# Decay factors through device memory in a gated delta-rule tower on one TensorE

## The reference

```python
h = tokens(x)                                  # patches @ W + b, class token first
z = layernorm(h)                               # factor r = 1 / sqrt(var + 1e-5), one for each token
q, k, v = silu(conv4(z @ Wq)), silu(conv4(z @ Wk)), silu(conv4(z @ Wv))
alpha, beta = sigmoid(z @ Wa), sigmoid(z @ Wb) # one of each for each token
for t in tokens:                               # state S: 128 x 128 for each image
    S = alpha[t] * (S - beta[t] * (S @ k[t]) k[t]^T) + beta[t] * v[t] k[t]^T
    o[t] = S @ q[t]
h = h + (rmsnorm(o) * silu(z @ Wg)) @ Wo       # q and k are l2-normed
h = h + ffn(layernorm(h))                      # mixed weights, about the last 200 us
```

## Time and profile before

| | |
|---|---|
| three executions, us | 844.44, 844.86, 850.1 (median 844.86) |
| the profiled execution, us | 845.34 |
| its span, first to last instruction, us | 843.3 |
| outside the span, us | 2.04 |
| PE busy | 819.7 us, 97% |
| DVE, ACT, POOL busy | 77%, 59%, 43% |
| start of the gates in step -1, 0 and 1, us | 23.18, 38.04, 60.03 |
| step 11, from level 1 of the inverse to that of step 12 (L1325 to L1325), us | 24.16 |

### The profile page before, as it was taken

One profiled execution on the slowest core, in us unless ns is written; L12 is line 12 of the kernel. 1 busy time (PEld: TensorE's weight loads), 2 busy tenths in 40 slices (PEclk: granted clock), 3 DMA queues, 4 the chain that ended last, 5 costly groups with the idle time before them and its releaser, 6 DMA issues.

```text
span 843.3 us, 31784 instructions
## 1 busy us (share of the span) xinstructions
PE 819.7 (97%) x12142; PEld 650.3 (77%) x12142; DVE 646.1 (77%) x2314; ACT 499.5 (59%) x1773; POOL 364.8 (43%) x530
## 2 busy tenths in 40 slices
PE   9899999999999999999999999999998999999996
PEld 7777787787877877878778778787787777777775
DVE  5467888888888888888888888888785977777434
ACT  1446565666766656567666566666644466666664
POOL 3123433333344233333442332333312398888775
PEclk7999999999999999999999999999999999999999
DMA  2001112222211011011111111111012133333331
GB/s 67 16 13 29 42 53 61 58 51 63 63 50 46 26 37 34 25 38 38 36 35 27 35 35 26 38 33 33 28 53 75 51 113 113 113 113 113 113 113 45
DMA packets 78661, 45.37 MB, mean 54 GB/s; under 512 B 20357, under 2 KB 69803, under 8 KB 78511
## 3 DMA queue, kind: packets, MB, share of 16 engines
q1 hardware_dynamic: 77663, 42.80, 18.2%
q10 hardware_dynamic: 848, 0.54, 0.2%
HBM read 23.69 MB, written 19.63 MB: 51 GB/s over the span
## 4 chain that ended last, share of the span: by engine, by line
PE 92%; DVE 5%; issue 2%; ACT 1%; POOL 0%; DVEq 0%; ACTq 0%; POOLq 0%
PE bank L2174 10%; PE bank L2148 9%; PE bank L1412 7%; PE bank L1413 5%; PE bank L1325 5%; PE bank L1349 5%; PE bank L1368 3%; PE bank L1506 3%; PE bank L1483 3%; PE bank L1542 3%; PE bank L1435 3%; PE bank L1369 3%; PE bank L1561 3%; PE bank L1517 2%; PE bank L1474 2%; PE bank L1546 2%
## 5 line engine op out<-in xcount | busy, mean ns | idle before, releaser
L2174 PEld LDWEIGHTS bank<-work 128*128 128x128 f32 x768 | 89.6, 192 | 12.0 <-issue 11.8
L2046 ACT ACTIVATE work<-bank,b1mix 128x512 f32<-128x512 f32 x96 | 65.7, 688 | 54.9 <-PE bank L2148 54.9
L2174 PE MATMUL bank<-work 128*128 128x128 f32 x768 | 89.9, 275 | 0.4 <-DVE work L1914 0.4
L2148 PE MATMUL bank<-work 128*128 128x512 f32 x192 | 86.6, 593 | 0.0
L494 ACT ACTIVATE work<-bank 128x512 f32<-128x512 f32 x50 | 29.9, 597 | 94.3 <-PE bank L1413 94.3
L764 POOL TENSOR_SCALAR var2e<-mv 128x4 f32<-128x4 f32 x22 | 5.0, 229 | 166.8 <-DVE mv L973 166.8
L1412 PE MATMUL bank<-SA,work 128*128 128x256 f32 x200 | 67.1, 417 | 0.0
L2148 PEld LDWEIGHTS bank<-work 128*128 128x128 f32 x192 | 34.6, 190 | 34.1 <-issue 34.0
L1413 PE MATMUL bank<-SB,work 128*128 128x256 f32 x200 | 59.5, 379 | 0.0
L1325 PEld LDWEIGHTS bank<-work 32*32 32x32 f32 x3200 | 35.0, 107 | 31.5 <-issue 25.7
L1961 DVE TENSOR_TENSOR work<-bank,work 128x512 f32<-128x512 f32 x24 | 16.6, 691 | 53.4 <-PE bank L2174 53.4
(11 more groups left out here) (293 smaller groups left out, 2387.5 us busy)
## 6 DMA issues: line engine op xcount, KB each, us to landing
hn_kept<-work SPq DMA_DIRECT2D x25, 256.0 KB, 2.3
hnT_kept<-work SPq DMA_DIRECT2D x25, 256.0 KB, 2.3
work<-hnT_kept SPq DMA_DIRECT2D x25, 256.0 KB, 3.0
work<-hn_kept SPq DMA_DIRECT2D x25, 256.0 KB, 3.2
out_dram<-work SPq DMA_DIRECT2D x24, 256.0 KB, 2.5
tv<-in_L_ffn_tv_W_dram SPq DMA_DIRECT2D x16, 256.0 KB
work<-r_kept SPq DMA_DIRECT2D x25, 98.0 KB
work<-in_x_dram SPq DMA_DIRECT2D x23, 102.0 KB
```

Source lines behind the costliest of these rows:

```text
L2046: ins = nc.scalar.activation(hid[f][:, :], ps[:, :], ACT.Relu, bias=b1mix[:, of[0], f:f + 1])
L2148: ins = mm(ps[:, :], w1T[of[0]][:, f, :], ghT[par][:, :, :].rearrange("p t c -> p (t c)"), start=True, stop=True)
L2174: ins = mm(by4(bank[2 + par])[:, t, :], hid[f][:, t * C:(t + 1) * C], w2T[of[t]][:, f, :], start=(f == 0 and t == 0), stop=(f == FB - 1), ...
```

## The change

Four things are done.

1. The alphas take the way of the norm factor. `rstd1` and `ab0` become the two halves of one 128 x 8 tile (`columns`); one transposition (`rows`) makes 8 rows of them, ACT copies 8 rows, SP writes 8 rows to device memory (`rows_kept`), and a new transfer reads the four alpha rows back to all 128 partitions (`alpha`, 256 KB). DVE's scan reads that tile and no longer bank 2. The four transpositions `alpha_rows` go from every step but -1, where they remain under the name of the fill.
2. For this the order within a step is changed on all five engines: POOL takes the exponent first, then the first norm's factor, then the second's; DVE takes the first norm's statistics and the alphas before level 2, and the second norm's later; PE makes the rows after the product with the inverse (L1474), and in the second half of a step the key transposition and level 5 come ahead of the state's product (L1517); SP writes the rows ahead of `hn`.
3. In step -2 the first product with the biases moves ahead of the factor's transposition, `keep_busy(4)` there goes, and `keep_busy(12)` after the folding becomes `keep_busy(3)`.
4. In step -1 the alphas are made right after the keys' and values' products, ACT squares the keys between its two copies, and DVE scales the next patches after `Bm` instead of before it.

The diff, cut to its core:

```diff
@@ SP
+                if on(j, LE) or on(j, LF):
+                    n = j + LE
+                    sp.wait_ge(r_row_ready, n + 1)
+                    sp.dma_start(rows_dram[n], rrows[0:2 * NB, 0, :]).then_inc(r_out, 16)
+                    sp.wait_ge(r_out, 16 * (n + 1))
+                if on(j, LF) and j > first + 1:
+                    s = j + LF
+                    need(sp, decay_ready, s)
+                    sp.dma_start(alpha[:, :], rows_dram[j + LE, NB:2 * NB, :].rearrange("b c -> (b c)").partition_broadcast(D)).then_inc(alpha_in, 16)
+                if on(j, LE):
...
+                    sp.dma_start(rrows[64:64 + PIX + 1], rows_dram[s, 0:NB, :].partition_broadcast(PIX + 1)).then_inc(rrows_in, 16)
...
@@ ACT
+                if j == first + 1:
+                    act.wait_ge(kvg_ready, 2)
+                    key_squares((0, 1))
                 kv_out(1)
+                if j == first + 1:
+                    act.wait_ge(kvg_ready, 3)
+                    key_squares((2, 3)).then_inc(ssk_ready, 1)
...
+                def rows_out():
+                    if on(j, LE) or on(j, LF):
+                        n = j + LE
+                        act.wait_ge(r_row_ps, n + 1)
...
+                        nc.scalar.copy(rrows[0:rows, 0, :], bank[7][0:rows, 0:C]).then_inc(r_row_ready, 1)
+
+                if j != first + 1:
+                    rows_out()
@@ DVE
-                    nc.vector.tensor_tensor_scan(decay.rearrange("p b c -> p (b c)"), bank[2][:, :],
+                    if j == first + 1:
+                        dve.wait_ge(alpha0_ps, 1)
+                    else:
+                        dve.wait_ge(alpha_in, 16 * s)
...
+                    nc.vector.tensor_tensor_scan(decay.rearrange("p b c -> p (b c)"), (bank[2] if j == first + 1 else alpha)[:, :],
...
                     nc.vector.tensor_tensor(Bm[p], by4(bank[4]), cdecay, ALU.mult).then_inc(B_ready, 1)
 
+                    if j == first + 1:
+                        scaled_patches()
@@ PE
-                keep_busy(4)
+                pe.wait_ge(proj_in, 16 * len(projection))
+                mm(bank[5][:, 0:256], onehot2, bias_row[:, 0:256], start=True, stop=False)
...
                 pe.wait_ge(r_row_ready, 1)
-                keep_busy(12)
+                keep_busy(3)
...
-                def alpha_rows():
-                    if F_:
-                        pe.wait_ge(ab0_ready, s1 + 1)
-                        need(pe, decay_ready, s1)
-                        for b in range(NB):
-                            ins = tr(by4(bank[2])[:, b, :], ab0[:, b:b + 1].broadcast_to([D, D]), ident[:, :])
-                        ins.then_inc(alpha_ps, 1)
+                def rows():
+                    if E_ or F_:
+                        if E_:
+                            pe.wait_ge(rstd1_ready, e + 1)
+                        if F_:
+                            pe.wait_ge(ab0_ready, s1 + 1)
...
+                        tr(bank[7][0:2 * NB, 0:C], columns[:, :], ident[:, :]).then_inc(r_row_ps, 1)
...
+                if not fill:
+                    rows()
                 if I_:
                     level_blocks(3, s0)
...
                 if fill:
                     pe.wait_ge(kvg_ready, KV_PARTS * s1 + 1)
-                    factor_row()
+                    pe.wait_ge(ab0_ready, 1)
+                    for b in range(NB):
+                        ins = tr(by4(bank[2])[:, b, :], ab0[:, b:b + 1].broadcast_to([D, D]), ident[:, :])
+                    ins.then_inc(alpha0_ps, 1)
+                    pe.wait_ge(rstd1_ready, e + 1)
+                    tr(bank[7][0:NB, 0:C], rstd1[:, :], ident[:, :]).then_inc(r_row_ps, 1)
                     key_columns()
-                    queries()
-                    alpha_rows()
-                else:
-                    queries()
-                    factor_row()
+                queries()
```

More of the change, by code:

```diff
@@ L155, in vit_tower @@
         sq = tile(NB * D, NB, D)
-        sq_q = tile(NB * D, NB, D)
+        sq_q = sq
+        alpha = tile(NB * C)
         sq_o = tile(NB * D, NB, D)
@@ L168, in vit_tower @@
         var1e = sb("var1e", [D, NB])
-        rstd1 = sb("rstd1", [D, NB])
+        columns = sb("columns", [D, 2 * NB])
+        rstd1, ab0 = columns[:, 0:NB], columns[:, NB:2 * NB]
         logit = sb("logit", [D, 8])
@@ L401, in body @@
                     ffn["load_tv"](sp, j - TV_FROM)
+                if on(j, LE) or on(j, LF):
[8 more added lines that the diff above has]
+                if on(j, LE):
+                    s = j + LE
+                    if s == 0:
+                        sp.wait_ge(rrows_set, 1)
+                    need(sp, xs_ready, s)
+                    sp.dma_start(rrows[64:64 + PIX + 1], rows_dram[s, 0:NB, :].partition_broadcast(PIX + 1)).then_inc(rrows_in, 16)
+                    sp.dma_start(rrows[64 + PIX + 2:64 + KX], rows_dram[s:s + 1, 0:NB, :]).then_inc(rrows_in, 16)
+                if j == first:
+                    ffn["load"](sp)
                 if on(j, LH):
@@ L959, in body, with keep_h0 @@
                     grow(1, j + LI)
+                if j == first:
+                    center_weights()
+                if on(j, LE):
+                    s = j + LE
+                    def keep_h0():
+                        if s == 0:
+                            dve.wait_ge(bo_in, 16)
+                        h = h1buf[:, :, bass.ds(s, 1), :].rearrange("p b s c -> p b (s c)")
+                        nc.vector.tensor_tensor(h, by4(bank[1]), bo_rows[:, :].unsqueeze(1).broadcast_to([D, NB, D]), ALU.add).then_inc(h0_kept, 1)
+                    dve.wait_ge(h0_ps, s + 1)
+                    need(dve, mv1_ready, s)
+                    for b in range(NB):
+                        ins = nc.vector.bn_stats(stats1[:, b, :], by4(bank[1])[:, b, :])
+                    ins.then_inc(stats1_done, 1)
+                    if s == 0:
+                        fold_weights()
+                    dve.wait_ge(stats1_done, s + 1)
+                    need(dve, var1e_ready, s)
+                    for b in range(NB):
+                        ins = nc.vector.bn_aggr(mv1[:, b, :], stats1[:, b, :])
+                    ins.then_inc(mv1_ready, 1)
+                    if s == 0:
+                        keep_h0()
+                        output_weights()
@@ new lines, in body @@
+                if on(j, LI):
+                    new_blocks(2, j + LI)
+                if on(j, LE) and j > first:
+                    s = j + LE
+                    keep_h0()
+                if on(j, LI):
+                    s = j + LI
+                    dve.wait_ge(kvg_ready, KV_PARTS * (s + 1))
+                    need(dve, vmean_ready, s)
+                    nc.vector.tensor_reduce(vsum[:, :], kvg[s % 3][:, :, D:2 * D], AX.X, ALU.add).then_inc(vsum_ready, 1)
+                if on(j, LI):
+                    grow(2, j + LI)
@@ L1513, in body @@
                     query_rows()
+                if not fill:
+                    key_columns()
+                if I_:
+                    level_blocks(5, s0)
                 if C_:
@@ L1520, in body @@
                     keep_busy(3, 6)
-                if not fill:
-                    key_columns()
-                if I_:
-                    level_blocks(5, s0)
-                if not fill:
-                    alpha_rows()
                 if H_:
```

179 lines of the change are left out of this document (66 added, 113 removed).

## The result

The changed kernel took 833.1 us, median of 4 runs (830.73 to 834.5), against 845.4 (844.44 to 850.1) on the same chip: 12.3 us less, ratio 0.985 with a 95% interval of 0.9818 to 0.9881. The forecast was 830.7, range 826.5 to 837. The profiled execution is the fastest of the four, 830.73 with a span of 828.7: its span is 14.6 us under that of before (843.3), the forecast's sum to the tenth.

| term | forecast | measured between the two profiles |
|---|---|---|
| keys and values of step -1 done | 2.4 earlier | 28.29 to 23.63: 4.66 |
| from there to level 1 of step 0 | 1.2 | 9.37 to 8.12: 1.25 |
| steps 0 to 23 and what follows | 11.0 | 8.7 |

A forecast was written before the change was run, and what follows sets the result against it. PE's own sequence was taken to bound the kernel, with DVE as tight from level 6 on. Loop 11.0, fill 2.4 and step -1's order 1.2 sum to 14.6 us off 845.34: 830.7, range 826.5 to 837.

The forecast's parts named there:

- steps 0 to 23 and what follows: The loop: 24 steps each 0.47 us shorter, less 0.27 for step 23, together 11.0 us saved.
- The alpha transpositions: PE in steps 0 to 23: removing the group L1398, a slot of 0.48 us, saves 0.47 a step.
- 0.48 if PE decides: Upper end of the saving per step: PE's slot from L1398 to the next group; 0.25 if something new takes half.
- the deduction was 0.12: Step 23, which had no row transposition, gets one on PE; the forecast charged its duration, 0.27 us.
- Does DVE follow?: DVE at level 5's copy: its 0.50 us wait for L1328 closes, so its second half moves up by 0.47.
- the tie of L1144 and level 1: DVE's transposition L1144 ends 0.14 us before PE's level 1 starts; so from level 6 DVE is as tight as PE.
- DVE becomes the bound: Rival, chance 0.14: DVE has no pause left from level 4's mask to level 6; 0.25 a step, 836.0 us, pitch 23.9 or more.
- The alphas late: Rival, chance 0.06: the alphas' read lands after its 2.6 us cover, the scan waits, each step pays one for one; 854.7 at 1.0.
- The fill: Steps -2 and -1: fewer constant products start the gates at 17.1 instead of 23.25; keys and values done 2.4 us earlier.
- the first: Outcome taken for the fill: clock rises at 23.8 again, keys and values done at 25.9, 2.4 us earlier.
- The rival with a rise later than before: Clock stays low for longer in the fill, chance 0.13: 832.7 us, or 834.3 if queries and key products are slow too.
- Step -1's order: Alphas ahead of the queries gain 1.85 us, patches' product behind `Bm` costs 0.69; net 1.2, between 0.5 and 1.9.

The follow-up runs named there:

- product_ahead: The changed kernel with the state's product back in its old place, ahead of the keys' transposition and level 5's blocks: 836.37 us in one run, pitch 23.93.
- late_alphas: The changed kernel with SP reading the alphas only behind `hn`'s write and the wait for its landing: 855.62 us in one run.
- two_relus_earlier: The changed kernel with two of ACT's four relus moved ahead of level 6's copy: 828.11 us, ratio 0.9808 to the kernel before.
- folding_alone: The kernel before with only the folding's part: first bias product earlier, no 4 fillers there, 3 instead of 12 behind the folding: 843.23 us, ratio 0.9971.

## Why the prediction was right, and where not

**The alpha transpositions: 0.47 a step, measured 0.39.** That PE's slot is the price, and not their copies or waits, is shown (0.44 back for 0.44 put in). The step that failed is "0.48 if PE decides": it priced the removed group and not its neighbours. With the alphas went the place of the state's product, which moved behind the 32x32 group and costs 1.00 instead of 0.89 there. 0.48 - 0.10 is the 0.38 that PE's rows show. 24 x 0.39 = 9.4; four longer steps take 0.6 of it, two of them in both profiles, and I have no cause for them. The deduction of 0.27 for step 23 was too large: from its level 1 to that of the drain it went from 23.72 to 23.45, 0.27 less, so the deduction was 0.12. The row transposition takes 0.20 there to the next start, and the product with the inverse ahead of it 0.09 less than before.

**"Does DVE follow?"** The copy moved by the 0.47 that was worked out, and with no pause before it. But the question was put wrongly. I read the tie of L1144 and level 1 as DVE setting the step from level 6 on. What ended the step in the changed kernel was a chain on from PE's L1600: the gated output's copy, four relus, then the gates, 3.17 us (363.04 - 359.87). The kernel before has the same chain from L1570 and the same pause, but no run tested it there. DVE had 0.25 to spare at its end, as product_ahead and late_alphas showed by absorbing, and two_relus_earlier by gaining. The rows given stop at level 1's start, one row short of the pause.

**DVE becomes the bound**, the rival: by its own mark (23.9 or more) it didn't happen in the changed kernel. The price that it named as unknown, the scan's other source, is 0.09 and lay in that slack.

**The alphas late**: they weren't. The estimate of 3.2 from `hn`'s read the earlier trace rows was 3.5 on the page, and the median cover 2.5 instead of 2.6. But single writes lost some 2 us and left 0.06 to 0.4 of the cover, so in those steps the rival was near. The price beyond the cover is now measured: the wait less 0.38.

**The fill: 2.4, measured 4.66.** The gates' start was forecast to 0.4 us; the size hung on when the clock rises, and "the first" of three outcomes was taken where the second came: a rise at 21.2 (24.3 forecast for 20.7, measured 23.63). The amount of work at the lower clock, 10.8, was wrong as well. With the time behind the rise counted double, the stretch from the gates to the end of keys and values makes 9.4: (21.19 - 16.68) + 2 x (23.63 - 21.19) in the changed kernel's profile, and (23.81 - 16.98) + 2 x (25.09 - 23.81) in product_ahead's. The latter is the first outcome itself, a rise at 23.8, and it gives 3.2 instead of 2.4.

Over all 14 profiles here the rise came between 19.2 and 21.2 in ten and between 22.7 and 23.8 in four, whichever kernel it was. With three filling products the term is therefore 4.6 to 5.4 or 3.2 to 3.7, by the execution. The folding alone gave only 2.5 in the medians. The lower stretch behind PE's pause takes 1.7 back in its profiles, but without it the median was the same, so the rest stays open. The rival with a rise later than before did not come up. The Trainium skill, TensorE: Matmul & The Clock Gate, "What's actually happening", says that the default is the throttled clock and that activity releases it. The fall behind PE's pause of 1.68 us in folding_alone, and its absence with the pause filled, agree; the kernel before has the same pause and no fall. That fewer filling products would put the rise off is not borne out: with three it came at 21.2, with twelve at 23.8 in the kernel before and at 19.6 in the changed one.

**Step -1's order: 1.2, measured 1.25**, and for the reason given: 2.0 for the alphas' place (1.85 forecast) less 0.72 for the patches' product (0.69).

So the 830.7 of the profiled run is a sum of two errors, 2.3 too little in the fill and 2.3 too much in the loop. That they cancel is luck: the two profiles compared differ in when the clock rose, at 23.8 and at 21.2. The median stands 2.4 above it. As a rough check, with the folding's 2.5 from medians in place of the 4.66, the terms are 2.5 + 1.25 + 8.7 = 12.4, near the 12.3 between the medians.

## What to carry to other kernels

A group taken out of a busy engine is worth its slot less what its neighbours then cost: count from start to start across the whole stretch, with the new neighbours' prices from a place where the same pair stands already. To say which engine ends a step, read one row past the tie and look for the engine's own pause; a pause of 0.25 in each step was worth more than any theory about DVE. And when a fill is made shorter, look at the granted clock behind the pauses that remain: here a lower stretch took back 1.7 of 4.88 us.

## What the runs showed of the hardware

- A group of 8 full-size products takes, from its start to the next one's, 0.89 us between full-size groups, 0.98 to 1.00 with a 32x32 or 64x64 group on one side, and 1.09 with a 32x32 group on both. (The last product of a step, L1483, is left out, since what follows it also waits for DVE's L1177.) Four transpositions take 0.44 between full-size groups, 0.47 to 0.49 behind a 32x32 group and 0.53 ahead of one.
- The scan over 512 columns takes 1.31 to 1.32 us in all 23 steps of the changed kernel in which POOL's copy L811 runs beside its first 0.24 us, and 1.22 in every step of product_ahead and late_alphas in which POOL's copy isn't beside it. Both its operands are now tiles of the kind that POOL reads and writes (`work`, `ident`); before, one was in a bank, and the two scans with POOL at work beside them (a copy for 0.12 us, a power for 1.01) took 1.22. The Trainium skill, GPSIMD Engine Reference, "1. Specifications", names contention with VectorE instructions that have two SBUF inputs; these runs agree, with 0.09 us as the price for the scan when the copy is running already. In step 0 of the changed kernel one of POOL's copies starts 0.07 behind the scan. There the scan takes 1.22 and the copy pays: it takes 1.24 instead of 0.29 and ends 0.08 behind the scan. All nine profiles of the changed kernel and its edits show it in step 0, eight with a copy of 1.24, product_ahead with a power of 1.94 instead of 1.01. The view of the copy's line (count, shortest, median and longest in ns):

```profile
L811 POOL COPY work<-work x96: 283/287/1240, 46.4 to 592.1; 32x128 f32<-32x128 f32 x96
```

- A dependent write and read through device memory take 1.25 us from issue to issue in most steps, and up to 3.7 in single ones; the read of 256 KB takes 3.5 to landing (3.3 to 4.0 in the changed kernel's profile), beside the other transfers of a step.
- Lower stretches of the granted clock appear behind the recurrence too (between 634 and 647 us in four profiles), at some 1 us each.
